# Three products of zeros open each group of accumulator banks in the adjacency build of a graph and transformer kernel

## The reference

```
agg = jax.ops.segment_sum(norm[:, None] * x[row], col, num_segments=n)
...
alpha = p / (s[dst] + 1e-16)
out = jax.ops.segment_sum(alpha[:, :, None] * h[src], dst, num_segments=N)
```

## Time and profile before

| what | value |
|---|---|
| median of 3 runs | 3148.31 us (3144.77 to 3156.2) |
| the profiled execution, time | 3156.52 us |
| its span, first to last instruction | 3154.8 us |
| mean granted clock of PE in it | 0.90 of full |
| PE busy over the span | 2602.8 us (83%) |
| VectorE busy over the span | 1977.4 us (63%) |
| first visit of the build | at 23.80 us |
| last copy-out (L373) of the build | ends at 258.0 us |
| first load of the next phase | at 270.03 us |

### The profile page before, as it was taken

The page is one execution under the profiler, slowest core; times in us unless marked ns, Lnnn a source line. Parts: engine busy times, 40 slices in busy tenths (PEclk is TensorE's granted clock), DMA queues, the critical chain, the costliest instruction groups (busy, mean ns, idle before and its releaser), DMA issues. The chain is left out here.

```text
span 3154.8 us, 40044 instructions
## 1 busy us (share of the span) xinstructions
PE 2602.8 (83%) x14620; PEld 2311.3 (73%) x14621; DVE 1977.4 (63%) x2803; ACT 1386.1 (44%) x2313; POOL 356.7 (11%) x309
## 2 busy tenths in 40 slices
PE   5774888887986977975899689789897998999876
PEld 5763778887986977973888557367665776999766
DVE  7886287777867853345655343542895556989654
ACT  0343267775865831110566410031796103777330
POOL 1351040040030000001233210000000000111000
PEclk9986988998998988996999869879998997999978
DMA  0012101111111253221899750124561222444304
GB/s 33 20 41 67 62 10 62 53 41 51 52 43 43 70 135 80 44 64 57 264 251 256 186 127 0 49 88 150 139 130 37 83 64 51 107 93 86 92 1 103
DMA packets 107250, 267.13 MB, mean 85 GB/s; under 512 B 11062, under 2 KB 49448, under 8 KB 106090
## 3 DMA queue, kind: packets, MB, share of 16 engines
q1 hardware_dynamic: 99474, 238.26, 27.9%
q0 software_dynamic: 7616, 26.74, 3.9%
HBM read 194.41 MB, written 66.73 MB: 83 GB/s over the span
## 5 line engine op out<-in xcount | busy, mean ns | idle before, releaser
L902 PE MATMUL ps<-h,e_gat_aggregate 125*125 125x193 f32 x2400 | 404.9, 332 | 52.5 <-DVE e_gat_aggregate L884 52.5
L902 PEld LDWEIGHTS ps<-h,e_gat_aggregate 125*125 125x125 f32 x2400 | 398.7, 191 | 58.7 <-DVE e_gat_aggregate L884 58.7
L882 DVE TENSOR_TENSOR e_gat_aggregate<-e_gat_aggregate 125x1250 f32<-125x1250 f32 x120 | 174.7, 1456 | 77.9 <-ACT e_gat_aggregate L853 74.7
L103 PE MATMUL ps<-gat_w_pair_gat_scores,x_turned 128*125 128x384 f32 x1080 | 195.7, 344 | 32.1 <-DVE gat_w_pair_gat_scores L749 32.1
L103 PE MATMUL ps<-w_pair_dense_rows_from,col_dense_rows_from 128*125 128x384 f32 x1080 | 208.8, 351 | 16.2 <-DVE w_pair_dense_rows_from L1075 13.4
L103 PEld LDWEIGHTS ps<-gat_w_pair_gat_scores,x_turned 128*125 128x125 f32 x1080 | 194.5, 190 | 33.1 <-DVE gat_w_pair_gat_scores L749 32.9
L103 PEld LDWEIGHTS ps<-w_pair_dense_rows_from,col_dense_rows_from 128*125 128x125 f32 x1080 | 195.9, 194 | 17.9 <-issue 14.7
L850 ACT ACTIVATE e_gat_aggregate<-row_gat_aggregate,from_src 125x1250 f32<-125x1250 f32 x120 | 161.7, 1347 | 87.6 <-PE ps L902 62.5
L2437 DVE TENSOR_TENSOR ln_home<-p_attend,p_high_attend 125x1254 fp32r<-125x1254 f32 x120 | 182.7, 1535 | 26.9 <-ACT p_high_attend L2423 24.1
L2415 ACT ACTIVATE p_attend<-ps 125x1254 f32<-125x1254 f32 (+2 forms) x168 | 148.7, 915 | 79.6 <-PE ps L2378 77.7
L1930 DVE TENSOR_SCALAR_CACHE_REDUCE res_attention_statistics<-ps 125x1250 f32<-125x1250 f32 x120 | 173.0, 1459 | 12.7 <-PE ps L1907 7.4
(11 more groups left out here) (387 smaller groups left out, 5189.9 us busy)
## 6 DMA issues: line engine op xcount, KB each, us to landing
stock<-in_moe_w SPq DMA_DIRECT2D x34, 1152.0 KB, 7.0
row_gat_aggregate<-r_scratch SPq DMA_DIRECT2D x24, 625.0 KB, 6.1
V_home<-q_scratch SPq DMA_DIRECT2D x44, 312.5 KB, 6.3
ln_home<-q_scratch SPq DMA_DIRECT2D x36, 312.5 KB
ln_home<-k_scratch SPq DMA_DIRECT2D x36, 312.5 KB
rows_dense_rows_from<-node_scratch SPq DMA_DIRECT2D x8, 1080.0 KB
q_scratch<-V_home SPq DMA_DIRECT2D x6, 1250.0 KB, 4.6
k_scratch<-V_home SPq DMA_DIRECT2D x6, 1250.0 KB, 4.8
```

Source lines behind the costliest of these rows:

```text
L103: last = pe.matmul(out, left(x), right(y), start=start and n == 0, stop=stop and n == 2)
L882: v.tensor_tensor(e[:, n % 3, 0, :], e[:, n % 3, 0, :], e[:, n % 3, 1, :], ALU.max).then_inc(p_step, 1)
L902: last = pe.matmul(ps[0:TP, bank(head, d // 2), d % 2 * (C + 1):(d % 2 + 1) * (C + 1)], e[:, n % 3, 0, d * TP:(d + 1) * TP], h[:, t, head, :],
```

## The change

GpSimd writes a new array `zeros` (125 x 512 bf16) among the constants. In each window PE, after its wait for `staged` and ahead of its wait for the first one-hots, does three products of zeros, one for each bank, 512 columns wide, with `start=True`. No other product of the window has `start=True` now.

```diff
+    zeros = ph.sb("zeros", [TP, BANK], BF16)
     adj = ph.sb("adjacency", [TP, NT, NPAD])
...
             pool.memset(ones[:], 1.0)
+            pool.memset(zeros[:], 0.0)
             pool.memset(chain[:], 1.0)
...
                     pe.wait_ge(s["staged"], w + 1)
+                    for b in range(3):
+                        pe.matmul(ps[0:TP, 3 * odd + b, :], zeros[:, 0:TP], zeros[:], start=True, stop=False,
+                                  skip_group_check=True)
                     for j in range(2):
                         pe.wait_ge(first_ready[j], w + 1)
-                        visit(1 - odd, first_hot, j, odd, j == 0).then_inc(first_free[j], 1)
+                        visit(1 - odd, first_hot, j, odd, False).then_inc(first_free[j], 1)
```

## The result

The changed kernel takes 3170.7 us (median of 6 runs, 3166.1 to 3180.1) against 3152.3 us for the kernel before in the same number of runs: a ratio of 1.0065, 95% interval 1.0052 to 1.0079, or +20 us (16 to 25); the two medians themselves are 18.4 us apart. The forecast was 3160 on a median of 3148.3, within a range up to 3173: slower was right, and the move was about 1.7 times as large as said. It is over the bound of 0.5%, to which I had given 0.35.

A forecast was written before the change was run, and what follows sets the result against it. PE and VectorE taking turns bound the build early, mostly VectorE, slowed by GpSimd, late. Terms: +17 at full clock, -5 and +1 for the clock, +13, taken as +12: 3160 us on 3148.3, range 3150 to 3173.

The forecast's parts named there:

- The sum before the clock: Adjacency build at full clock: early windows +9.3, late windows +7.4 and memset +0.4 give +17 us.
- One group: Three products of zeros on PE in one window: 0.65 us at full clock, ends 0.55 and 0.72.
- Window 0: First window: zeros hidden in PE's 6.95 us idle time before its first visit; cost 0, or 1.3 us without it.
- The memset: GpSimd's write of the zeros before PE starts: 0.4 to 0.8 us, almost all on the path; +0.4 us.
- Early windows: Windows 1 to 17: each group added in full, 11.1 us, less 0.8 and 1.0 hidden; +9.3 us.
- the 0.28 that was to stay: Windows 1 to 17: VectorE's waits for PE's visits stay the same, with the same 0.28 us.
- Late windows: Windows 18 to 39: 14.3 us less what hides while visits wait for VectorE; +7.4 us, bounds 3 and 14.3.
- The clock: PE's seven half-clock spells in the build, worth about 10 us: added PE work wins back half, -5 us.
- +1 against it: Window entries still in a half-clock spell: groups cost 0.65 us more, partly hidden by VectorE's waits; +1 us.
- The clock pays for it: Rival for the build: all half-clock spells go, -10 us, net +4, 3152 us; chance 0.18.
- faster: Rival: full clock for the first visits, all spells gone, groups at 0.55 us, sum about -1; faster by 0.5%: chance 0.04.
- No cover and no clock: Rival: zeros added at all 39 windows, 25.4 us, clock spells staying; 3170 to 3178 us, chance 0.34.

The follow-up runs named there:

- early zeros alone: Changed kernel with PE's loop split in two and the zeros only in windows 0 to 17; 1.0051 (+16 us) against the kernel before.
- Narrow zeros: Changed kernel with the three products of zeros 128 columns wide, not 512; 0.9997 (-1 us) against the kernel before.
- the run with the even zeros ahead: Changed kernel with even windows' zeros issued at the end of the turn before, ahead of PE's register load; 1.0027 (+8.5 us) against the kernel before.
- The pair without sums: Kernel before and changed kernel, each with GpSimd's work in the windows reduced to one small copy; medians 3128.3 and 3151.3 us.
- The late half timed alone: Changed kernel with PE's loop split in two and the zeros only in windows 18 to 39; 1.0022 (+7 us) against the kernel before.
- the constant alone: Changed kernel without the three products, banks opened by their first product as before, memset kept; 1.0006 (+2 us) against the kernel before.
- ones there: Kernel before plus three 512-column products of ones into unused banks at each PE loop turn's end, before the register load; 0.9981 (-6 us).

## Why the prediction was right, and where it was off

**The direction was right, and so was its cause.** The products stand on PE's path, in series with the visits, and they cost time there. The sum before the clock was +17: 9.3 early, 7.4 late, 0.4 for the memset. That the time then fell inside the range is in part luck. Two terms were off against each other: the late windows cost less than said, and the clock took where it was to give.

**One group: right.** 0.65 us predicted, 0.65 measured (121.15 to 121.80). The row decided over the page: the 131 ns a product of the Trainium skill ("TensorE: Matmul & The Clock Gate", section "Back-to-back issue gap") would have been 0.39, an estimate.

**Window 0: wrong, small.** I put it at nothing. PE gets past its register load only at 23.68, not two microseconds before the one-hots, and the three products at half clock take 1.33 us, of which 0.75 show.

**The memset: right.** 0.46 us on the path, 0.4 said.

**Early windows: right at full clock, for a partly wrong reason.** I let each odd and even window carry its 0.65, less what hides. In fact the delay turns the order of VectorE and GpSimd. Where the pair is short, an odd window grows by more than 0.65 and an even one, at full clock, gets shorter: with early zeros alone window 9 takes 7.38 us instead of 5.94, and window 10 takes 5.04 instead of 5.45. VectorE's wait for PE is 0.81 us there and not the 0.28 that was to stay. Narrow zeros, 7 us of the same serial time, cost nothing in such a pair, which simple addition doesn't give. Each pair of early windows ran at full clock in one or another of the profiles with zeros. From these the early zeros come to about 10 us, an estimate (1.5, 1.8, 1.7, 1.0, 1.0, 1.0, 0.8 and 1.7 for the eight pairs, less 0.5 in window 17; windows 7 and 8 are from the run with the even zeros ahead). The pair without sums gives 8.7.

**Late windows: the mechanism was right, the size too high.** They give room because VectorE is late there, and most of that room comes from GpSimd. At an equal clock of 0.96 the late zeros cost 2.3 us in the profiles, against the term's 7.4 and its lower bound of 3. The late half timed alone, +7 with an interval from 3.5, would bear the 7.4 out. Its profile doesn't, and this stays open. One reading was wrong: the 1.03 us of window 28 in the earlier trace rows are PE's idle time, ended by ScalarE's copy-out, and not a distance from the window before.

**The clock: the step that failed.** "I take it that half of the loss comes back: -5", and +1 against it. Nothing came back. At half clock the kernel before spent about 31 us of the build from window 1 on, the changed one 34 and 38 us in its two profiles. Late the clock did come to the 0.95 that I had named (0.96); early it fell. What I missed is where. In the early part the time at half clock went from about 10 to 27 us, and there PE is on the chain: the part grew by 18.1 and 17.3 us, where the same zeros at full clock cost about 10. The other 8 us are the clock's. That is borne out by windows 9 and 10, which take 13.73 us in the changed kernel with a spell at the even entry and 12.42 without one. Late, the profile of the changed kernel has 2.7 us less of the clock's cost than that of the kernel before, but so has the profile of the constant alone. So the terms of the two profiles are 0.65 for the later start of window 1, 10 + 8 early and 2.3 - 2.7 late, which is the 18.3 us by which the last visit moved. The clock's net is some +5 where the forecast had -4.

Why the spells come more often in the early part is argued and not isolated. The zeros of an even window stand in front of the first visits, behind the idle time and not in it, and those of the odd window make the waits before it longer. Zeros moved into the idle time did raise the early clock from 0.89 to 0.96 (+8.5 us and not +20), and ones there (-6) left the build with as little time at half clock, 10 us. But the same waits were also seen without a spell.

**The rivals.** "The clock pays for it" and "faster" are out. "No cover and no clock" has the right size and half of the right reason: the clock gave nothing, but the cover was there.

## What to carry to other kernels

Work added to an engine that takes turns with another costs its own time only where it stands between the two; put it into the engine's idle time (here a loop's register load) and it may even pay, by the clock. A forecast of the clock needs the place as well as the amount: ask which wait the new work lengthens, and whether the engine behind it is on the chain where the clock falls. Read the clock from several profiles: the late windows without added products had 0.87 to 0.96 here. And take a small delay's price from the slack and not from the sum: 0.18 us a window cost nothing, 0.65 cost 20 us, 1.3 cost 29.

## What the runs showed of the hardware

The clock never fell in 168 and 186 us of build once GpSimd's sums were left out, though PE did the same products as with them. What the sums change for PE is the pace of VectorE; which of PE's waits brings the clock down was not isolated. In a pair of early windows one spell at half clock made 12.42 us into 13.73. VectorE's three-input operation of 128 columns took 344 ns alone and 501 to 509 ns on average beside GpSimd. A GpSimd memset of 125 x 512 bf16 took 0.52 us, where one of 128 x 128 f32 took 0.20.
